# Another order of the steps in the quantized feed-forward stage of a one-core graph transformer kernel

## The reference, cut to what matters

```python
def rmsnorm(x):
    return x * jax.lax.rsqrt(jnp.mean(x * x, axis=-1, keepdims=True) + EPS)
def act_quant(x):
    scale = 127.0 / jnp.clip(jnp.max(jnp.abs(x), axis=-1, keepdims=True), 1e-05)
    q = jnp.clip(jnp.round(x * scale), -128.0, 127.0) / scale
    return x + jax.lax.stop_gradient(q - x)
def bitlinear(x, w, b):
    xq = act_quant(rmsnorm(x))
    wq = weight_quant(w)
    return jnp.einsum('bsd,fd->bsf', xq, wq) + b
h = bitlinear(x, w1, b1)          # 1024 -> 512
h = jax.nn.gelu(h, approximate=False)
return bitlinear(h, w2, b2)       # 512 -> 1024
...
x = x + _L0_gnn_ref(...) + _L0_mix_ref(...)
x = x + _L0_ffn_ref(_layernorm(x, axis=-1)[None], ...)[0]
xn = _layernorm(x, axis=-1)
x = x + _L1_gnn_ref(xn, ...) + _L1_mix_ref(xn[None], ...)[0]
```

## Time and profile before

| | us |
|---|---|
| median of 3 runs | 812.29 (811.17 to 814.89) |
| profiled execution, its own time | 813.54 |
| its span (from the first to the last instruction) | 811.8 |
| PE busy | 779.2 (96% of the span) |
| DVE busy | 588.9 (73%) |
| ACT busy | 384.9 (47%) |

### The profile page before, as it was taken

The page is one execution under the profiler, slowest core; times in us unless marked ns, Lnnn a source line. Parts: engine busy times, 40 slices in busy tenths (PEclk is TensorE's granted clock), DMA queues, the critical chain, the costliest instruction groups (busy, mean ns, idle before and its releaser), DMA issues. The chain is left out here.

```text
span 811.8 us, 11521 instructions
## 1 busy us (share of the span) xinstructions
PE 779.2 (96%) x4270; PEld 689.5 (85%) x4270; DVE 588.9 (73%) x1242; ACT 384.9 (47%) x798; POOL 50.3 (6%) x86
## 2 busy tenths in 40 slices
PE   5999999999999899999997599999999989999998
PEld 5888878889999899998875388888888879999886
DVE  8988879646544788997699849789896686665331
ACT  5222123454434576765757536585574323464220
POOL 3000000000000000001103211000002021000000
PEclk9999999999999899999999899999999999999999
DMA  5522123332334323329965329234134236344331
GB/s 191 181 75 78 53 88 121 128 130 79 130 129 127 95 72 98 91 83 312 267 255 109 102 70 260 101 128 155 54 105 124 72 110 156 128 133 141 127 135 39
DMA packets 28775, 102.17 MB, mean 126 GB/s; under 512 B 3736, under 2 KB 3864, under 8 KB 28464
## 3 DMA queue, kind: packets, MB, share of 16 engines
q1 hardware_dynamic: 24784, 86.76, 32.2%
q0 software_dynamic: 3936, 14.68, 8.2%
HBM read 91.99 MB, written 1.57 MB: 115 GB/s over the span
## 5 line engine op out<-in xcount | busy, mean ns | idle before, releaser
L1175 DVE TENSOR_TENSOR w_lo<-raw,w_hi 128x1024 fp32r<-128x1024 f32 x140 | 169.9, 1222 | 65.5 <-ACT w_hi L892 65.0
L892 ACT ACTIVATE w_hi<-raw 128x1024 fp32r<-128x1024 f32 x140 | 147.3, 1058 | 111.2 <-PE bank L1932 83.6
L1881 PE MATMUL bank<-xn1T,w_hi 128*128 128x384 f32 x448 | 115.2, 338 | 0.0
L1932 PE MATMUL bank<-w_hi,xn3T 128*128 128x512 f32 x288 | 92.0, 393 | 0.0
L1881 PEld LDWEIGHTS bank<-xn1T,w_hi 128*128 128x128 f32 x448 | 80.0, 188 | 0.8
L1881 PE MATMUL bank<-xn1T,w_lo 128*128 128x384 f32 x224 | 75.0, 335 | 0.0
L1881 PE MATMUL bank<-xn4T,w_hi 128*128 128x384 f32 x256 | 65.3, 335 | 0.4 <-DVE xn4T L1166 0.4
L1932 PEld LDWEIGHTS bank<-w_hi,xn3T 128*128 128x128 f32 x288 | 54.1, 188 | 11.0
L1932 PE MATMUL bank<-w_lo,xn3T 128*128 128x512 f32 x144 | 56.0, 389 | 0.0
L1881 PEld LDWEIGHTS bank<-xn4T,w_hi 128*128 128x128 f32 x256 | 46.1, 188 | 0.6 <-DVE w_lo L1175 0.6
L1881 PE MATMUL bank<-xn4T,w_lo 128*128 128x384 f32 x128 | 42.8, 335 | 0.0
(11 more groups left out here) (352 smaller groups left out, 1694.9 us busy)
## 6 DMA issues: line engine op xcount, KB each, us to landing
raw<-weights SPq DMA_DIRECT2D x140, 512.0 KB, 3.3
row_sb<-rows SPq DMA_DIRECT2D x6, 512.0 KB, 6.1
kcat<-kcat POOLq DMA_DIRECT2D x16, 192.0 KB, 3.0
base<-rows POOLq DMA_DIRECT2D x6, 512.0 KB, 13.4
w2r<-w_in SPq DMA_DIRECT2D x1, 2048.0 KB, 9.4
w1r<-w_in POOLq DMA_DIRECT2D x1, 2048.0 KB, 9.2
x_sb<-x_in SPq DMA_DIRECT2D x3, 512.0 KB, 4.3
row_sb<-rows SPq DMA_DIRECT2D x6, 256.0 KB, 4.8
```

Source lines behind the costliest of these rows:

```text
L892: act.activation(w_hi[:, u % RING], raw[:, u % RAW], ACT.Copy).then_inc(hi_split, 1)
L1175: dve.tensor_tensor(w_lo[:, u % RING], raw[:, u % RAW], f(w_hi[:, u % RING]), ALU.subtract).then_inc(unit_split, 1)
L1881: last = pe.matmul(out_of(pr)[:, 0:N], w[pa][:, slot, k * P:(k + 1) * P], TT[src][:, pb, k], start=(k == 0 and m == 0), stop=(k == KD - 1 ...
L1932: last = pe.matmul(out_of(pr)[:], tile[:, pa, k, ts], w[pb][:, at_, j * HALF:(j + 1) * HALF], start=(kk == 0 and j == 0 and m == 0 and nam ...
```

## The change

The two long lists of steps between the output projection and the first product of layer two are replaced by another order of the same steps, and the third tile's inner transposes get bank 2 instead of 7. No instruction is added or removed. The list's first line is shown, before and after; what the orders do on the engines stands below it. Lines behind the list are one higher after the change (L2019 becomes L2020).

```diff
-    steps.extend([tiled("wo", 1, 0), ("gelu_table",), tiled("wo", 1, 1), ("in_stats", 0), ("w_cast", 0), ("in_amax", 0),
...
+    steps.extend([tiled("wo", 1, 0), ("in_stats", 0), ("in_amax", 0), tiled("wo", 1, 1), ("in_factor", 0),
...
         elif kind == "h_T":
-            product(f"hqT.{s[1]}", 7 - s[1] % 2)
+            product(f"hqT.{s[1]}", (7, 6, 2)[s[1]])
```

More of the change, by code:

```diff
@@ new lines, in schedule @@
+    steps.extend([tiled("wo", 1, 0), ("in_stats", 0), ("in_amax", 0), tiled("wo", 1, 1), ("in_factor", 0),
+                  tiled("wo", 1, 2, 0, 2), ("in_stats", 1), ("w_cast", 0), ("in_amax", 1), ("in_factor", 1),
+                  ("in_scale", 0), ("in_round", 0), tiled("wo", 1, 2, 2, 4), ("gelu_table",), ("in_scale", 1), ("in_T", 0),
+                  ("in_round", 1), ("in_stats", 2), ("in_amax", 2), ("in_factor", 2), ("ahead_hi",), ("in_T", 1),
+                  ("in_ev", 0), ("ffn_h", 0), ("in_ev", 1), ("hn", 0), ("ahead_hi",), ("in_scale", 2), ("in_round", 2),
+                  ("ffn_h", 1), ("hn", 1), ("gelu", 0), ("in_T", 2), ("square", 0), ("in_ev", 2), ("h_max", 0),
+                  ("h_factor", 0), ("h_round", 0), ("gelu", 1), ("ahead_lo",), ("h_max", 1), ("ffn_h", 2), ("h_cast", 0),
+                  ("h_T", 0), ("h_factor", 1), ("hn", 2), ("square", 1), ("h_ev", 0), ("gelu", 2), ("h_round", 1),
+                  ("ffn_o", 0), ("h_cast", 1), ("h_max", 2), ("h_factor", 2), ("x_out", 0), ("h_T", 1), ("square", 2),
+                  ("h_round", 2), ("h_ev", 1), ("ahead_hi",), ("ffn_o", 1), ("h_cast", 2), ("h_T", 2), ("x_out", 1),
+                  ("x_norm", 0), ("h_ev", 2), ("xn3_T", 0), ("ahead_hi",), ("ahead_lo",), ("ahead_lo",), ("xn3_hi", 0),
+                  ("ffn_o", 2), ("x_norm", 1), ("xn3_T", 1), ("xn3_lo", 0)])
@@ L182, in schedule @@
     run("g1", 0, 4)
-    steps.extend([tiled("g1", 0, 0, 0, 2), ("xn3_hi", 1), ("xn3_lo", 1), tiled("g1", 0, 0, 2, 4), ("x_norm", 2), ("xn3_T", 2),
-                  tiled("g1", 0, 1, 0, 2), ("xn3_hi", 2), ("xn3_lo", 2), tiled("g1", 0, 1, 2, 4), ("g1_out", 0),
-                  tiled("g1", 0, 2, 0, 2), tiled("g1", 0, 2, 2, 4), ("g1_out", 1), ("ahead",), ("ahead",), ("g1_out", 2)])
+    steps.extend([tiled("g1", 0, 0, 0, 2), ("ahead_lo",), ("x_out", 2), ("xn3_hi", 1), ("xn3_lo", 1),
+                  tiled("g1", 0, 0, 2, 4), tiled("g1", 0, 1, 0, 2), ("x_norm", 2), ("xn3_T", 2), tiled("g1", 0, 1, 2, 4),
+                  ("xn3_hi", 2), ("xn3_lo", 2), ("g1_out", 0), tiled("g1", 0, 2, 0, 2), tiled("g1", 0, 2, 2, 4),
+                  ("g1_out", 1), ("ahead",), ("ahead",), ("g1_out", 2)])
```

## The result

| | us |
|---|---|
| before, median of 11 runs | 812.49 (809.54 to 817.04) |
| after, median of 11 runs | 808.96 (806.98 to 811.56) |
| ratio, with 95% interval | 0.9957 (0.9939 to 0.9974) |
| profiled execution after, own time and span | 808.96 and 807.2 |

The change makes the kernel 3.5 us faster; the interval goes from 2.1 to 5.0 us. The forecast was 809.2.

A forecast was written before the change was run, and what follows sets the result against it. DVE's work and waits were taken to set `xn3_T(1)`'s start, and so the launch's time: −1.14 −0.38 −1.67 −0.60 +0.70 = −3.09, from a median of 812.29 to 809.2 us, range 806.9 to 812.0.

The forecast's parts named there:

- The split (1.14): On DVE, one of two weight splits moves behind `xn3_lo(0)`: minus 1.14 us.
- The wait of 0.38: DVE's wait for the output projection's last tile goes, as tile 1's rounding now comes first: minus 0.38 us.
- The wait of 1.67: DVE's wait for `gelu(1)` at `h_max(1)` goes, as ACT's load-bound weight step moves behind `h_ev(1)`: minus 1.67 us.
- The wait of 0.60: DVE's wait for `ffn_o(1)` at `x_out(1)` goes, since only tile 1's work stands before that product: minus 0.60 us.
- The new wait: DVE waits at `in_round(2)` for ACT's `in_scale(2)`, with only `hn(0)` covering it: plus 0.70 us.
- The costs put at nothing: Gelu table load, `h_max(2)`, bank 2, `x_out(2)`, SP's load permissions and POOL's reordered factors: each covered, no cost on the path.
- a long fall behind `xn3_T(1)`: Half-rate clock behind `xn3_T(1)`; each further 3.41 us costs 1.7, giving up to 814.3 us; chance 0.05.
- The clock at the start of `g1`: Rival: TensorE's clock stays up there behind a shorter gap, winning 1.7 us more, 807.5 us; chance 0.22.
- the row's state kept: Main case: clock at `g1`'s start stays low as in the earlier profile; gain 3.1, 809.2 us; chance 0.52.
- Part is given back by `ffn_o(2)`: Rival: this product, now ahead of `xn3_T(1)` on TensorE, delays it; with `h_max(2)` up to 1.5 lost, 810.7; chance 0.14.
- Nothing: Rival: the gain is swallowed behind the stage by weights that come no earlier; 812.3 us; chance 0.07.
- slower: Rival: TensorE's clock falls for long; from 6.2 us more low clock it decides, up to 814.3 us; chance 0.05.

The follow-up runs named there:

- Both weight steps alone: Seventh kernel: kernel before, fourth high part moved behind `h_ev(1)`, second low part behind `xn3_lo(0)`; 809.02 against 812.33, ratio 0.9955.
- the bank alone: Eighth kernel: kernel before with only the third tile's inner transposes in bank 2 instead of 7; 813.16 against 812.33, ratio 1.0006.
- the input part alone: Second kernel: kernel before with the changed order up to `ffn_h(1)`, the old order behind it; 812.22 against 811.78, ratio 1.0000.
- first: Kernel before with only the fourth high part moved from in front of `ffn_h(2)` to behind `h_ev(1)`; 810.47 against 811.78, ratio 0.9979.
- sixth: Kernel before with extra matmuls, results never read, in TensorE's gaps at seven places; 810.96 against 812.33, ratio 0.9981.
- twelfth kernel: Kernel before with one high and one low part moved later, plus unread matmuls at seven places; stage 35.36 us, time not shown to differ from the change.
- the first and the third of the last four kernels: Changed kernel plus unread matmuls: 12 ahead of `in_T(2)` and `ffn_h(2)`; or 38 in the stage's gaps and 6 ahead of `ffn_mean(0)`. Equally fast; latter's profiled execution 805.42.
- the third tile back: Changed kernel with tile 2's rounding, transposes and product back ahead of tile 0's and 1's output steps; 810.41 against 811.78 before, ratio 0.9978.
- the high parts early: Changed kernel with its third high part moved behind `in_ev(2)`, its fourth in front of `h_cast(0)`; 814.65 against 811.78 before, ratio 1.0041.

## Why the prediction was right, step by step

The total was right (3.1 us forecast, 3.5 measured), and its mechanism holds in the main. One term was a different thing from what I took it for, and one cost was missing; they have opposite signs. That the total came so near is thus in part luck: the profiled stage became 1.93 shorter, at full rate it is 2.6, and the interval of the times, 2.1 to 5.0, holds all of these.

1. **The split (1.14).** Right, as far as the waits tell, with a price at the old place. The times don't separate it: the intervals of one weight step (0.9961 to 0.9997) and of both (0.9938 to 0.9972) overlap. Both weight steps alone against the bank alone, the two profiles without a fall that DVE felt: 35.35 against 37.54, 2.19 us shorter. The terms give 1.14 + 1.67 − 0.70 = 2.11.
2. **The wait of 0.38** is gone in every kernel with the new input part; without it, it stands (0.36 to 0.47). Right, but beside step 5 worth nothing: −0.38 +0.65, and the input part alone brought no time.
3. **The wait of 1.67** is the main thing. Moving one high part alone removes it and brings 1.3 us (0.2 to 3.2 by the interval); putting it, and the one ahead of it, back in the changed order costs 3.35 us of wait and, by the medians, 5.7 us of time (3.86 of it in the profiled stage).
4. **The wait of 0.60: the step that failed.** "It goes" was true, "`ffn_o(1)` has only tile 1's work before it" was not the reason. The 3.50 us for eight matmuls in the earlier trace rows is half rate, and in the six other profiles with the old order's inner products (the first, second, sixth, seventh, eighth and twelfth kernel) it ran at full rate and no such wait exists. The prediction itself calls it a half-rate product where it speaks of the clock, but books its wait as the order's. It is a cost that one execution has and another hasn't; as a term of the change it is worth nothing that the runs show.
5. **The new wait** was put at 0.70 and measured 0.65, in all eight kernels with the new input part.

Missing from the sum: the new order's own fall of the clock, at 440.35 in the profile. It costs 0.54 + 0.16 + 0.86 = 1.56 us at `hn(2)` and `x_out(0)`. I had looked at this gap for a long fall behind `xn3_T(1)` only, and had counted `x_out(1)`, not `x_out(0)`, as the reader of a slow product. At full rate the sum closes without steps 4 and this one: −1.14 −0.38 −1.67 +0.70 = −2.49, and the measured stages are 34.9 (the first and the third of the last four kernels) against 37.5 (the order before, filled, and the bank alone), −2.6. The median's 3.5 is some 1 us more than that, which isn't accounted for, but the interval allows it.

**The costs put at nothing** were nothing: 0.47 us spare at the table (forecast 0.5), no wait at `h_max(2)` and `x_out(2)`, POOL 1.46 and 0.76 as before, bank 2. In front of `xn3_T(1)` TensorE was idle 2.22 us (forecast 2 to 2.7); it started at 460.02, below the 460.5 to 462.5 given, because the stage began 2.57 earlier. Counted from `w_cast(0)` it was 1.2 us later than the sum says.

**The rivals.** The clock at the start of `g1` was 0.51 for 3.41 us in spite of the shorter gap, so the row's state kept was the better choice. Both falls came behind short gaps: one of 2.08 us in front of `in_T(2)` (in the profiles of the change, of the third tile back and of the high parts early alike), one of 2.22 in front of `xn3_T(1)`, each of them among several with little work between. The same gap of 2.09 in the second kernel had no fall behind it until 447.8, 6.5 us later. The Trainium skill ("TensorE: Matmul & The Clock Gate", "Why this matters for your kernels") advises against idle gaps between bursts. The trace of before agrees with its gap of 3.54; the gaps of 2.08 and 2.22 here are shorter than those that the page warns of, and the clock fell behind them all the same, so the longest gap alone doesn't decide. Where fillers kept the clock up at `g1`, the rest was 1.5 us shorter (343.9 to 342.4), and from the start of `xn3_T(1)` on it was 1.5 as well (344.8 to 343.3), against 1.7 as I had priced it. "Part is given back by `ffn_o(2)`": that product ended at 457.81, far ahead. "Nothing" and "slower": no; the clock was low for 6.8 us more than before (10.24 against 3.40 inside the stage), which the slower rival had priced at 3.4 us, but it lay ahead of `xn3_T(1)`, where it costs only what DVE waits.

**What stays open.** The change's parts beyond the weight steps (input part, transposes, third tile, bank) shorten the stage by some 0.45 at full rate (35.35 to 34.9) and bring the inner fall, which costs more in the profile (36.26). The medians, 809.02 and 808.96, tell no difference. How often each fall occurs in executions without a profile isn't known; their mean granted clock is 0.993 for the order before (81 runs) and for the change (11 runs), with mean times of 812.2 and 809.1: at the same mean clock 3.1 us apart. The filled kernels' profiles promise up to 2.9 us more than the change has (1.4 in the stage, 1.5 behind it), their medians show 0.6. For the kernel filled only ahead of `g1` the 1.25 us that its fillers cost is a reason; why the others show so little isn't settled.

## What to carry to other kernels

Put an operation that needs a load behind the work that hides the load's landing (here 3.3 us from issue), and not behind its permission: on an engine that works in order everything queued behind it waits too, and putting two of them back there cost more than the whole change had brought. Moving two weight steps alone was here worth as much as the whole reordering. When a wait is entered in a sum, look first whether its producer ran at full rate: compare the same shape elsewhere (1.90 against 3.5 to 3.6 us here), since a wait for a half-rate product can be gone in another execution whatever the order. Where work between two long bursts gets sparse, a few matmuls that nobody reads kept the clock up here, but expect far less from them than the stretch at half rate suggests, and see that they end before the work that the path waits for.

## What the runs showed of the hardware

- **The clock's fall has no fixed place.** With the same order of steps it was low from 454.7 in one profile (before) and from 446.5 in another (the bank alone, which differs in one bank). The changed order's inner fall lasted 10.24 us in its own profile and 3.4 in that of the kernel filled only ahead of `g1`, whose instructions are the same up to that point. With `g1`'s gap alone filled, it fell at 457.8, in front of the place that it had.
- **A fall far ahead of the change goes with most of the difference between profiles.** Up to `w_cast(0)` the kernels do nearly the same, and yet it started between 423.1 and 426.8 in 14 profiles. Without a low clock near 277 (after, high parts early, bank alone, and the change filled at the mean too) it started at 423.1 to 423.8; where it was low for 6.8 us there (before and four more) at 426.0 to 426.8; for 3.4 us at 424.5 to 426.8. Two of the latter (426.8 and 425.8) had a further fall at about 419. This was read from the profiles, not tested by a kernel.
- **POOL's small operation beside DVE.** The same 128x1 operation (L826) took 1.46 us for tile 1 and 0.55 for tile 2, in the kernel after as before; for tile 0 0.81:

```profile
452.27 0.81 POOL L826 TENSOR_TENSOR rstd<-var,minus_half 128x1 f32<-128x1 f32 x1 [7.44 <-DVE var L1198]
...
456.38 1.46 POOL L826 TENSOR_TENSOR rstd<-var,minus_half 128x1 f32<-128x1 f32 x1 [2.02 <-DVE var L1198]
...
464.24 0.55 POOL L826 TENSOR_TENSOR rstd<-var,minus_half 128x1 f32<-128x1 f32 x1 [5.54 <-DVE var L1198]
```

  The long one lies beside two splits on DVE (2.35 us from 456.22 on). In all 14 profiles tile 1's takes 1.45 or 1.46, beside two splits on DVE, and in the two chains shown it is on the path with its 0.9 us too much. That the splits cause it isn't shown. Moving the splits away from it wasn't tried.
